# One-hot rows of later batches by eight narrow comparisons, tile one-hots one step later, and the first batch's masked gathers moved back

## The chip, the core and the metric

The kernel runs on one core of one Trainium2 chip. The metric is the device time of one execution in microseconds (us). Three runs of the kernel before gave a median of 1613.91 us (1612.84 to 1618.62). Of this kernel, half a per cent (about 8 us) is about what a measurement can tell from no change.

## The reference, cut to what matters

```python
# x: (16, 512, 1024), mask: (16, 1024) of 0 and 1, Wq and Wo: (512, 512)
xt = transpose(x, (0, 2, 1))                       # (B, T, D)
q = xt @ Wq.T
qh = q.reshape(B, T, 8, 64).transpose(0, 2, 1, 3)  # queries, keys and values are the same
scores = einsum('bhqd,bhkd->bhqk', qh, qh) / sqrt(64)
logits = (scores * cmask + (1 - cmask) * -1e30) * rmask
ctx = softmax(logits, axis=-1) @ qh
out = ctx.reshape(B, T, D) @ Wo.T
return x + transpose(out, (0, 2, 1))
```

A masked token is left out as a key. As a query, all its logits are zero, so its output is the mean of all tokens' values, one row for the whole batch.

## The kernel before, in words

**Tiles.** In each of the 16 batches the unmasked tokens are put first. They fit into 5 tiles of 108 rows (540 places, the form called "small"; the code also holds a form "middle" with 116 rows and a form "full", which these inputs don't use). The masked tokens follow in 5 tail tiles. Gathers by GpSimd's indirect DMA fetch the rows of x in this order (`small_xg` for the first five tiles, `small_xtail` for the tail), by the row numbers in `small_idx`; scatters write them back.

**Row numbers.** `idx` of a batch is a product on TensorE (`late_order`, line 1138): for each of 8 token groups (TT = 8) a one-hot matrix of the row within a tile (`late_hot_row`, 128 x 108, fp16) times a one-hot of the tile, weighted with the token's number (`late_hot_tile`). The tile one-hots of all batches are made once by two VectorE operations (`hot_tiles`, lines 901 and 904). The row one-hots are made for one batch at a time by `hot_row_of(b)` (line 933), with two buffers: one comparison of 864 elements a partition between `late_rowno` and `late_jl`, both broadcast. Batch 1's is made before the main loop, those of batches 2 to 15 in batch 0, at the steps in `HOT_ROW_AT`. VectorE then turns each product into `small_idx` (line 940).

**Main loop.** A batch is 8 heads of 5 steps, and (h, k) is step k of head h. In a step TensorE computes two half tiles of scores for the row maxima of the head after next (`max_scores`, line 1182; two PSUM banks, each given back by a VectorE reduction, line 962), two half tiles of scores of this head (lines 1198 and 1201), the products with the values one head later (line 1213), and pieces of other work on two PSUM banks called misc: projections of later pairs of heads (line 1248), transposes, the orders, and from the second batch on the previous batch's output. ScalarE takes the exponentials (line 812). GpSimd adds up the exponentials for the softmax's sums (`add_tile`, line 634: `small_Pacc`, 108 x 540), sums tokens (line 622), makes the low parts of Wo in batch 0 (`wo_low`, line 608) and issues the gathers and scatters (lines 568 and 580). Each float32 operand is a high part (rounded, `small_H`) and a low part (the rest, `small_L`), for which reason VectorE subtracts (line 977) behind ScalarE's copy (line 733).

**Order.** Each engine's order is written out by tables of steps: `WO_HIGH_AT` (ScalarE's high parts of Wo, line 685), `WO_LOW_AT` (GpSimd's low parts), `GATHER_TAIL_AT`, `SCATTER_AT`, `HOT_ROW_AT` and `ORDER_AT`. Engines wait for each other by semaphores only. SyncE's queue carries the copies of the high and low parts into the operand slots (`small_ops<-small_H` and `small_L`, 6 of 135 KB a head).

**Front.** Before batch 0 the list `front_jobs` is worked off: five transposes, the projections (0, 0) and (0, 1) of the first pair of heads, the two value transposes V, the projections (1, 0) and (1, 1), with the order of batch 1 between them, then (2, 0), and the row maxima of heads 0 and 1. `hot_tiles` stands behind the low part of (0, 0), `hot_row_of(1)` behind that of (0, 1). The batches' numbers for VectorE (`late_jl`, `late_rowno`, `late_boff`) are copied ahead of that (line 926). The projection (2, 0) writes the same buffer of `small_H` as pair 0, so ScalarE waits there until the copies of heads 0 and 1 have landed.

Of the kernel before, what the change touches and what calls it, by code (L numbers as in the profile page):

```python
# [19 lines left out]
P = 128  # L20
F32 = mybir.dt.float32
F32R = mybir.dt.float32r
BF16 = mybir.dt.bfloat16
F16 = mybir.dt.float16
I32 = mybir.dt.int32
ALU = mybir.AluOpType
# [26 lines left out]
SCALE_AT = [(3, 0), (3, 1)]  # L53
MASKED_AT = [(0, 0), (0, 1)]

WO_HIGH_AT = [(0, 3), (0, 4), (1, 0), (1, 1)]
WO_LOW_AT = [(1, 3), (1, 4), (2, 0), (2, 1)]

ADD_W_AT = [(0, 0), (0, 1), (0, 3), (0, 4), (1, 0)]
SCATTER_TAIL_AT = [(1, 1), (1, 3), (1, 4), (2, 0), (2, 1)]  # L60
GATHER_TAIL_AT = [(2, 3), (2, 4), (3, 0), (3, 1), (3, 3)]
SCATTER_AT = [(3, 4), (4, 0), (4, 1), (5, 0), (5, 1)]
# [102 lines left out]
def pool_jobs(form, has_prev, has_next, has_third):  # L165


    NT, NTAIL = form.NT, form.NTAIL
    table = {(h, k): [] for h in range(HEADS) for k in range(NT)}
    steps = list(table)  # L170
    if form.split:
        for i in range(NTAIL):
            if has_prev:
                table[ADD_W_AT[i]].append(("add_w", -1, i))
                table[SCATTER_TAIL_AT[i]].append(("scatter", -1, NT + i))
            table[GATHER_TAIL_AT[i]].append(("gather", 0, NT + i))
            table[TAIL_SUM_AT[i]].append(("sum_tokens", 0, NT + i))
        for i in range(NT):
            if has_prev:
                table[SCATTER_AT[i]].append(("scatter", -1, i))  # L180
            if has_third:
                table[GATHER_AT[i]].append(("gather", 2, i))
        for i in range(1, NT):
            if has_next:
                table[SUM_AT[i - 1]].append(("sum_tokens", 1, i))
            if not has_prev:
                table[FIRST_SUM_AT[i - 1]].append(("sum_tokens", 0, i))
        if not has_prev:
            for i, at in enumerate(WO_LOW_AT):
                table[at].append(("wo_low", 0, i))  # L190
        return table
    scatters = [steps[steps.index(at) + 2] for at in FULL_OUT_AT]
    gathers = [max(steps[steps.index(at) + 2], (1, 4)) for at in scatters]
    if has_prev:
        for i, at in enumerate(scatters):
            table[at].append(("scatter", -1, i))
    if has_next:
        for i in range(NT):
            table[gathers[i]].append(("gather", 1, i))
    for i in range(1, NT):  # L200
        table[4 + (i - 1) // 3, (i - 1) % 3].append(("sum_tokens", 0, i))
    return table
# [97 lines left out]
def attention_kernel(nc, x_rows, mask_t, wq, wqT, woT, out_rows, B, T, D):  # L300
    KD = D // P
    TT = T // P
# [4 lines left out]
    with ExitStack() as ctx:  # L307
# [6 lines left out]
        def sem(name):  # L314
# [24 lines left out]
            g_kept, place_step, onehots_made, perm_made, idx_made, jidx_made, ops_cleared = sems.values()  # L339
# [41 lines left out]
        for f, t in zip(forms, tensors):  # L381
# [17 lines left out]
            def place_tables(stage, t=t, f=f):  # L399

                batches = 1 if f.split else B
                tables = ExitStack()
                for where, name, shape, dt in (
                        ("early", "hot_tile_f", [P, TT, B, f.NTALL], F32), ("early", "jh", [P, TT, B], F32),
                        ("early", "jl", [P, TT, B], F32), ("early", "tileno", [P, f.NTALL], F32),
                        ("early", "tileno_i", [P, f.NTALL], I32), ("early", "rowno", [P, f.R], F32),
                        ("early", "rowno_i", [P, f.R], I32), ("early", "jidx_i", [P, f.NTALL], I32),
                        ("early", "boff_i", [P, B, f.NTALL], I32), ("early", "boff", [P, B, f.NTALL], F32),
                        ("early", "hot_tile", [P, TT, batches, f.NTALL], F16), ("early", "hot_row", [P, TT, batches, f.R], F16),
                        ("late", "late_jl", [P, TT, B], F32), ("late", "late_rowno", [P, f.R], F32),  # L410
                        ("late", "late_boff", [P, B, f.NTALL], F32), ("late", "late_hot_tile", [P, TT, B, f.NTALL], F16),
                        ("late", "late_hot_row", [P, 2, TT, f.R], F16)):
                    if where == stage:
                        t[name] = sb(f"{f.name}_{name}", shape, dt, tables)
                tables.close()
# [433 lines left out]
        def _(dve):  # L849
# [25 lines left out]
            def body(f, t, plan):  # L875
# [52 lines left out]
                def hot_row_of(b):  # L928

                    if b == 1:  # L930
                        dve.wait_ge(place_step, NTALL + 8)
                    at_least(dve, perm_made, b - 1)
                    nc.vector.tensor_tensor(t["late_hot_row"][:, b % 2], t["late_rowno"][:].unsqueeze(1).to_broadcast([P, TT, R]),
                                            t["late_jl"][:, :, b].unsqueeze(2).to_broadcast([P, TT, R]),
                                            ALU.is_equal).then_inc(onehots_made, 1)

                def idx_of(b, bank):

# [121 lines left out]
                for name, arg, bank, before in plan[0]:  # L1060
# [3 lines left out]
                    job(name, arg, bank, -1 if name == "xT" else 0, 1 if name == "xT" else 0, 0)  # L1064
                    if f.split and (name, arg) == ("xT", NT - 1):
                        move_tables()
                    if f.split and (name, arg) == ("proj", (0, 0)):
                        hot_tiles(t["late_hot_tile"])
                    if f.split and (name, arg) == ("proj", (0, 1)):
                        hot_row_of(1)  # L1070
                for m in range(2 * NT):
                    reduce_max(1, 1, m)
# [342 lines left out]
```

## Time and profile before

| | |
|---|---|
| median of three runs | 1613.91 us |
| the profiled execution's own time | 1613.59 us |
| its span, first to last instruction | 1611.8 us |
| TensorE matmuls busy | 1535.3 us (95%) |
| VectorE busy | 1190.2 us (74%) |
| ScalarE busy | 854.6 us (53%) |
| GpSimd busy | 1340.9 us (83%) |
| granted TensorE clock, mean | 0.977 of full |

Busy shares are means over the whole span. The first batch and the front are where they say least, so stretches are read one by one below. Idle time of an engine that nobody waits for costs nothing. In the rows PE is TensorE's matmuls, PEld its weight loads, DVE VectorE, ACT ScalarE, POOL GpSimd.

### The profile page before, as it was taken

The numbers are of one execution on the slowest core, as the hardware profiler recorded it, in microseconds if no ns is written. First come the engines' busy times: TensorE is split into PE (matmuls) and PEld (weight loads), VectorE is DVE, ScalarE is ACT, GpSimd is POOL, SyncE is SP. The second block draws the span as 40 slices with busy tenths as digits, with TensorE's granted clock in tenths as the row PEclk, the third lists the DMA queues.
The fourth block names the chain that finished last, engine by engine and source line by source line (L and its number), as shares of the span: only waits on it lengthen the run. The fifth ranks groups of instructions, "written<-read, shape, count | busy, mean of one in ns | idle before, by whom it ended". The sixth has DMA issues, their size and how long they took to land. (4 is left out here: it accounts for less than half of the span.)

```text
span 1611.8 us, 33099 instructions
## 1 busy us (share of the span) xinstructions
PE 1535.3 (95%) x10956; PEld 1218.7 (76%) x10956; DVE 1190.2 (74%) x2676; ACT 854.6 (53%) x2061; POOL 1340.9 (83%) x1078
## 2 busy tenths in 40 slices
PE   5989999999999999999999999999999999999984
PEld 4668787778777777777777777877777787778753
DVE  4587787878778787877878787777878777787743
ACT  4345555555555555555555555555555555655440
POOL 3467889898988989898898989889898988988864
PEclk9889999999999999999999999999999999999987
DMA  4433354454535445454544455454445444443501
GB/s 136 103 84 88 94 131 102 124 122 115 136 93 132 99 121 123 121 130 97 128 104 120 117 128 123 103 127 107 118 115 131 117 110 120 113 118 88 134 18 54
DMA packets 93810, 179.09 MB, mean 111 GB/s; under 512 B 24704, under 2 KB 24832, under 8 KB 93632
## 3 DMA queue, kind: packets, MB, share of 16 engines
q1 hardware_dynamic: 64448, 109.71, 29.4%
q0 software_dynamic: 29184, 67.17, 15.1%
q8 instruction: 92, 1.51, 0.4%
q14 instruction: 86, 0.70, 0.1%
HBM read 36.77 MB, written 33.55 MB: 44 GB/s over the span
## 5 line engine op out<-in xcount | busy, mean ns | idle before, releaser
L962 DVE TENSOR_REDUCE small_mxp<-max_scores 108x1 f32<-108x270 f32 x1280 | 547.9, 436 | 266.7 <-PE max_scores L1182 243.3
L812 ACT ACTIVATE small_Pt<-scores,small_kbias 108x270 f32<-108x270 f32 x1280 | 551.5, 483 | 363.3 <-PE scores L1201 357.9
L634 POOL TENSOR_TENSOR small_Pacc<-small_Pacc,small_Pt 108x540 f32<-108x540 f32 x384 | 520.7, 1356 | 124.0 <-ACT small_Pt L812 117.5
L1182 PE MATMUL max_scores<-small_ops 128*108 128x270 f32 x1280 | 417.9, 333 | 16.0 <-DVE small_mxp L962 14.2
L1213 PE MATMUL ctx_psum<-small_Pt,small_V 108*64 108x270 f32 x2560 | 317.6, 395 | 0.0
L994 DVE RECIPROCAL small_rsum<-small_rsum 128x67 f32<-128x67 f32 (+1 forms) x512 | 240.7, 532 | 78.7 <-ACT small_rsum L748 73.4
L1182 PEld LDWEIGHTS max_scores<-small_ops 128*108 128x108 f32 x1280 | 220.6, 175 | 86.5 <-issue 42.1
L1198 PE MATMUL scores<-small_ops 128*108 128x270 f32 x1280 | 271.3, 292 | 2.7 <-ACT small_Pt L812 2.7
L1213 PEld LDWEIGHTS ctx_psum<-small_Pt,small_V 108*64 108x64 f32 x2560 | 186.1, 139 | 111.1 <-issue 5.7
L1201 PE MATMUL scores<-small_ops 128*108 128x270 f32 x1280 | 265.7, 289 | 0.0
L1198 PEld LDWEIGHTS scores<-small_ops 128*108 128x108 f32 x1280 | 192.9, 174 | 21.8 <-issue 8.3
L634 POOL TENSOR_TENSOR small_Pacc<-small_Pt 108x540 f32<-108x540 f32 x128 | 171.8, 1342 | 31.5 <-ACT small_Pt L812 28.9
L1201 PEld LDWEIGHTS scores<-small_ops 128*108 128x108 f32 x1280 | 192.7, 174 | 0.0
L1248 PE MATMUL misc<-small_xcT,small_wqT_hi 128*128 128x270 f32 x512 | 151.8, 297 | 13.2 <-DVE small_xcT_lo L986 12.1
L1248 PE MATMUL misc<-small_xcT_lo,small_wqT_hi 128*128 128x270 f32 x512 | 148.6, 290 | 0.0
L1248 PE MATMUL misc<-small_xcT,small_wqT_lo 128*128 128x270 f32 x512 | 147.9, 289 | 0.0
L1248 PE MATMUL misc<-small_woT_hi,small_ctxT 128*108 128x512 f32 x320 | 127.0, 397 | 6.2 <-DVE small_ctxT_lo L999 6.2
L1248 PE MATMUL misc<-small_woT_lo,small_ctxT 128*108 128x512 f32 x320 | 127.5, 398 | 0.0
L1248 PE MATMUL misc<-small_woT_hi,small_ctxT_lo 128*108 128x512 f32 x320 | 126.7, 396 | 0.0
L1017 DVE TENSOR_TENSOR small_ctx<-small_rsum,ctx_psum 64x270 f32<-64x270 f32 x256 | 110.5, 432 | 9.1 <-issue 3.3
L568 POOL DMA_INDIRECT small_xg<-x_rows,small_idx x80 | 85.1, 1063 | 37.9 <-issue 15.3
L709 ACT CAST small_xcT<-misc 128x432 fp32r<-128x432 f32 x80 | 41.7, 521 | 134.8 <-PE misc L1260 134.8
(115 smaller groups left out, 2365.2 us busy)
## 6 DMA issues: line engine op xcount, KB each, us to landing
small_ops<-small_H SPq DMA_DIRECT2D x512, 135.0 KB
small_ops<-small_L SPq DMA_DIRECT2D x256, 135.0 KB
small_ops<-small_mrow SPq DMA_DIRECT2D x128, 2.1 KB
small_xg<-x_rows,small_idx POOLq DMA_INDIRECT x80, 4.0
small_xtail<-x_rows,small_idx POOLq DMA_INDIRECT x80, 4.6
out_rows<-small_xtail,small_idx POOLq DMA_INDIRECT x80, 3.7
out_rows<-small_xg,small_idx POOLq DMA_INDIRECT x80, 3.8
wqT_sb<-wqT SPq DMA_DIRECT2D x1, 1024.0 KB, 5.4
```

Of the source, the lines that this page charges most:

```text
L568: nc.gpsimd.indirect_dma_start(out=tokens(f, t, b, k), out_offset=None, in_=x_rows, in_offset=bass.IndirectOffsetOnAxis(ap=t["idx"][:r, b, ...
L634: nc.gpsimd.tensor_tensor(acc, other, t["Pt"][:R, p0], ALU.add).then_inc(pacc_step, 1)
L709: nc.scalar.copy(t["xcT"][:, :, R * arg:R * arg + R], MB[bank][:, 0:KD * R].rearrange("p (c r) -> p c r", c=KD)).then_inc(xT_kept, 1)
L812: nc.scalar.activation(t["Pt"][:R, (NT * s + k) % f.NP, half, :], ST[(2 * (NT * h + k) + half) % 3][:R, 0:H], ACT.Exp, bias=t["kbias"][:R, ...
L962: nc.vector.tensor_reduce(t["mxp"][:R, h % 2, m // 2, m % 2:m % 2 + 1], MX[m % 2][:R, 0:H], AX.X, ALU.max).then_inc(mx_red, 1)
L994: nc.vector.reciprocal(t["rsum"][:, cols], t["rsum"][:, cols]).then_inc(recip_step, 1)
L1017: last = nc.vector.tensor_tensor(t["ctx"][pr:pr + DK, h // 2 % 2, cols] if f.split else t["ctxT"][pr:pr + DK, h // 2, cols], t["rsum"][r0: ...
L1182: nc.tensor.matmul(MX[m % 2][:R, 0:H], ops[:, OPA, tile_cols(m // 2)], ops[:, OPB, half_cols(m % 2)], start=True, stop=True).then_inc(mx_r ...
L1198: nc.tensor.matmul(banks[half][:R, 0:H], ops[:, OPA, tile_cols(k)], ops[:, OPB, half_cols(half)], start=True, stop=False)
L1201: nc.tensor.matmul(banks[half][:R, 0:H], ops[:, OPY, tile_cols(k)], ops[:, OPX, half_cols(half)], start=False, stop=True).then_inc(s_ready, 1)
L1213: last = nc.tensor.matmul(CT[DK * half:DK * half + DK, 0:H], t["V"][:R, (h // 2) % 2, k, DK * (h % 2):DK * (h % 2) + DK], t["Pt"][:R, (NT ...
L1248: last = nc.tensor.matmul(out, lefts[a][left_at], rights[z][right_at], start=(c == 0 and i == 0), stop=(c == KD - 1 and i == 2))
```

## The change: what it does

Three edits. (1) `hot_row_of` compares a fp16 row of 108 numbers (`late_rowno` is now fp16) with a number per partition, eight times, once for each token group; the semaphore moves with the last. (2) In the front both `hot_tiles` and `hot_row_of(1)` now stand behind the low part of projection (0, 1). (3) Steps are moved: in batch 0 the five gathers of the masked tail are issued at the steps of `SCATTER_AT`, where there is no scatter yet, the high parts of Wo move on ScalarE, and the low parts on GpSimd. Later batches keep their steps.

```diff
-WO_HIGH_AT = [(0, 3), (0, 4), (1, 0), (1, 1)]
-WO_LOW_AT = [(1, 3), (1, 4), (2, 0), (2, 1)]
+WO_HIGH_AT = [(0, 2), (0, 4), (1, 1), (1, 3)]
+WO_LOW_AT = [(1, 0), (1, 3), (2, 0), (2, 3)]
...
-            table[GATHER_TAIL_AT[i]].append(("gather", 0, NT + i))
+            table[(GATHER_TAIL_AT if has_prev else SCATTER_AT)[i]].append(("gather", 0, NT + i))
...
-                        ("late", "late_jl", [P, TT, B], F32), ("late", "late_rowno", [P, f.R], F32),
+                        ("late", "late_jl", [P, TT, B], F32), ("late", "late_rowno", [P, f.R], F16),
...
-                    nc.vector.tensor_tensor(t["late_hot_row"][:, b % 2], t["late_rowno"][:].unsqueeze(1).to_broadcast([P, TT, R]),
-                                            t["late_jl"][:, :, b].unsqueeze(2).to_broadcast([P, TT, R]),
-                                            ALU.is_equal).then_inc(onehots_made, 1)
+                    for tt in range(TT):
+                        last = nc.vector.tensor_scalar(t["late_hot_row"][:, b % 2, tt], t["late_rowno"][:],
+                                                       t["late_jl"][:, tt, b:b + 1], None, ALU.is_equal)
+                    last.then_inc(onehots_made, 1)
...
-                    if f.split and (name, arg) == ("proj", (0, 0)):
+                    if f.split and (name, arg) == ("proj", (0, 1)):
                         hot_tiles(t["late_hot_tile"])
-                    if f.split and (name, arg) == ("proj", (0, 1)):
                         hot_row_of(1)
```

**VectorE, the front.** The rows from the copy of `late_boff` on, before. `small_L` is the low part of a projection: (0, 0), (0, 1), (1, 0), then (1, 1) and (2, 0).

```order
L926 COPY small_late_boff<-small_boff 128x160
L977 TENSOR_TENSOR small_L<-misc,small_H 128x270
L901 TENSOR_TENSOR small_hot_tile_f<-small_tileno,small_jh 128x1280
L904 TENSOR_TENSOR small_late_hot_tile<-small_hot_tile_f,tokid 128x1280
L977 TENSOR_TENSOR small_L<-misc,small_H 128x270
L933 TENSOR_TENSOR small_late_hot_row<-small_late_rowno,small_late_jl 128x864
L977 TENSOR_TENSOR small_L<-misc,small_H 128x270
L940 TENSOR_TENSOR small_idx<-misc,small_late_boff 108x10
```

The same place in the changed kernel.

```order
L926 COPY small_late_boff<-small_boff 128x160
L978 TENSOR_TENSOR small_L<-misc,small_H 128x270 x2
L901 TENSOR_TENSOR small_hot_tile_f<-small_tileno,small_jh 128x1280
L904 TENSOR_TENSOR small_late_hot_tile<-small_hot_tile_f,tokid 128x1280
L934 TENSOR_SCALAR small_late_hot_row<-small_late_rowno,small_late_jl 128x108 x8
L978 TENSOR_TENSOR small_L<-misc,small_H 128x270
L941 TENSOR_TENSOR small_idx<-misc,small_late_boff 108x10
```

The low part of (0, 1) stands ahead of the tile one-hots now; one operation of 864 elements has become eight of 108.

**GpSimd, heads 1 and 2 of batch 0.** Before, from the last token sum of head 1's beginning on. A head has four adds into `small_Pacc`, of which the first reads `small_Pt` alone.

```order
L622 TENSOR_TENSOR small_xsum<-small_xsum,small_xg 108x512
L634 TENSOR_TENSOR small_Pacc<-small_Pt 108x540
L634 TENSOR_TENSOR small_Pacc<-small_Pacc,small_Pt 108x540 x2
L608 TENSOR_TENSOR small_woT_lo<-woT_sb,small_woT_hi 128x512
L634 TENSOR_TENSOR small_Pacc<-small_Pacc,small_Pt 108x540
L608 TENSOR_TENSOR small_woT_lo<-woT_sb,small_woT_hi 128x512 x2
L634 TENSOR_TENSOR small_Pacc<-small_Pt 108x540
L608 TENSOR_TENSOR small_woT_lo<-woT_sb,small_woT_hi 128x512
L634 TENSOR_TENSOR small_Pacc<-small_Pacc,small_Pt 108x540 x2
L568 DMA small_xtail<-x_rows,small_idx 108x512
```

The same heads in the changed kernel.

```order
L622 TENSOR_TENSOR small_xsum<-small_xsum,small_xg 108x512
L608 TENSOR_TENSOR small_woT_lo<-woT_sb,small_woT_hi 128x512
L634 TENSOR_TENSOR small_Pacc<-small_Pt 108x540
L634 TENSOR_TENSOR small_Pacc<-small_Pacc,small_Pt 108x540 x2
L608 TENSOR_TENSOR small_woT_lo<-woT_sb,small_woT_hi 128x512
L634 TENSOR_TENSOR small_Pacc<-small_Pacc,small_Pt 108x540
L608 TENSOR_TENSOR small_woT_lo<-woT_sb,small_woT_hi 128x512
L634 TENSOR_TENSOR small_Pacc<-small_Pt 108x540
L634 TENSOR_TENSOR small_Pacc<-small_Pacc,small_Pt 108x540 x2
L608 TENSOR_TENSOR small_woT_lo<-woT_sb,small_woT_hi 128x512
L634 TENSOR_TENSOR small_Pacc<-small_Pacc,small_Pt 108x540
```

The first low part of Wo has moved ahead of head 1's adds and the last one behind head 2's third; the gather of the tail is no longer in head 2.

## Rows read from the trace of the kernel before

**Rows 1.** The page: busy time of the engines, and the granted clock in 40 slices.
```profile
PE 1535.3 (95%) x10956; PEld 1218.7 (76%) x10956; DVE 1190.2 (74%) x2676; ACT 854.6 (53%) x2061; POOL 1340.9 (83%) x1078
...
PEclk9889999999999999999999999999999999999987
```

**Rows 2.** Busy time by windows, heads 0 to 4 of batches 0 and 1 (columns in the first line).
```profile
core 0: us, PE busy (x) PEld busy (x) DVE busy (x) ACT busy (x) POOL busy (x), PEclk, DMA share, GB/s
64.30:134.90 70.60, 60.88 (x469) 50.05 (x467) 57.55 (x119) 35.85 (x84) 47.41 (x34) 0.85 0.26 63
...
167.50:228.60 61.10, 60.38 (x440) 49.02 (x439) 48.69 (x107) 34.13 (x82) 51.93 (x43) 1.00 0.44 109
```

**Rows 3.** The same view, narrower windows of the front and batch 0.
```profile
80.00:100.00 20.00, 15.14 (x123) 11.92 (x119) 18.28 (x34) 7.52 (x18) 12.96 (x9) 0.83 0.20 44
100.00:120.00 20.00, 16.87 (x121) 12.65 (x121) 17.35 (x37) 8.37 (x21) 15.00 (x11) 0.80 0.45 114
120.00:140.00 20.00, 19.21 (x139) 15.90 (x140) 13.28 (x32) 11.34 (x28) 10.60 (x9) 0.86 0.25 60
88.00:90.00 2.00, 0.00 (x0) 0.00 (x0) 2.00 (x1) 0.00 (x0) 2.00 (x2) 0.51 0.55 122
42.00:44.00 2.00, 2.00 (x12) 2.00 (x12) 0.44 (x1) 0.38 (x1) 1.40 (x2) 0.59 0.91 226
```

**Rows 4.** The row one-hots, 0 to 150 us: busy us, mean ns; then min/median/max ns.
```profile
L933 DVE TENSOR_TENSOR small_late_hot_row<-small_late_rowno,small_late_jl 128x864 f16<-128x864 f32 x15 | 22.2, 1479 | 0.1
...
L933 DVE TENSOR_TENSOR small_late_hot_row<-small_late_rowno,small_late_jl x15: 1043/1068/4446, 33.2 to 117.7; 128x864 f16<-128x864 f32 x15
```

**Rows 5.** Timeline at 84 to 92 us: start us, duration us, engine, line; idle before in brackets.
```profile
85.41 1.27 POOL L608 TENSOR_TENSOR small_woT_lo<-woT_sb,small_woT_hi 128x512 fp32r<-128x512 f32 x1
85.65 4.45 DVE L933 TENSOR_TENSOR small_late_hot_row<-small_late_rowno,small_late_jl 128x864 f16<-128x864 f32 x1
...
86.65 1.32 POOL L634 TENSOR_TENSOR small_Pacc<-small_Pacc,small_Pt 108x540 f32<-108x540 f32 x1
...
87.93 3.30 POOL L608 TENSOR_TENSOR small_woT_lo<-woT_sb,small_woT_hi 128x512 fp32r<-128x512 f32 x2
...
90.24 0.88 PE L1138 MATMUL misc<-small_late_hot_tile,small_late_hot_row 128*108 128x10 f16 x8 [3.63 <-DVE small_late_hot_row L933]
```

**Rows 6.** Timeline, two other meetings of GpSimd's operations and the row one-hots.
```profile
73.94 2.31 POOL L634 TENSOR_TENSOR small_Pacc<-small_Pacc,small_Pt 108x540 f32<-108x540 f32 x1
73.98 1.05 DVE L933 TENSOR_TENSOR small_late_hot_row<-small_late_rowno,small_late_jl 128x864 f16<-128x864 f32 x1
...
107.11 1.00 POOL L568 DMA_INDIRECT small_xtail<-x_rows,small_idx  x1 [0.30 <-issue]
108.14 1.34 POOL L634 TENSOR_TENSOR small_Pacc<-small_Pt 108x540 f32<-108x540 f32 x1
108.16 2.24 DVE L933 TENSOR_TENSOR small_late_hot_row<-small_late_rowno,small_late_jl 128x864 f16<-128x864 f32 x1
```

**Rows 7.** Timeline of the front, 30 to 46 us, by engine.
```profile
30.62 0.38 ACT L733 CAST small_H<-misc 128x270 fp32r<-128x270 f32 x1 [1.11 <-PE misc L1248]
...
31.41 1.49 DVE L904 TENSOR_TENSOR small_late_hot_tile<-small_hot_tile_f,tokid 128x1280 f16<-128x1280 f32 x1
32.83 0.43 DVE L977 TENSOR_TENSOR small_L<-misc,small_H 128x270 fp32r<-128x270 f32 x1
...
33.40 0.41 PE L1296 MATMUL misc<-identR,small_H 128*108 128x128 f32 x1 [2.82 <-DVE small_L L977]
...
40.08 1.01 POOL L568 DMA_INDIRECT small_xg<-x_rows,small_idx  x1 [14.22 <-DVE small_idx L940]
...
45.47 0.39 ACT L733 CAST small_H<-misc 128x270 fp32r<-128x270 f32 x1 [2.22 <-DMA small_ops<-small_L]
```

**Rows 8.** Timeline of VectorE: short operations that follow each other without a wait.
```profile
27.25 0.21 DVE L926 COPY small_late_rowno<-small_rowno 128x108 f32<-128x108 f32 x1
...
27.38 0.24 DVE L926 COPY small_late_boff<-small_boff 128x160 f32<-128x160 f32 x1
...
90.56 0.16 DVE L940 TENSOR_TENSOR small_idx<-misc,small_late_boff 108x10 int32<-108x10 f32 x1
90.64 0.43 DVE L962 TENSOR_REDUCE small_mxp<-max_scores 108x1 f32<-108x270 f32 x1
```

## The prediction

> **What bounds the kernel now.** I read the page first. TensorE's matmuls are busy for 95% of the span, VectorE's work for 74%, and the granted clock is at its full level (2.4 GHz) in all slices but the first three and the last [rows 1]. So the long middle belongs to TensorE, and nothing in the change touches batches 1 to 15. What can move is the front and batch 0. Next I set heads 0 to 4 of batch 0 beside those of batch 1, by windows [rows 2]. Batch 0 takes 70.6 us for them, batch 1 61.1 us, though only batch 1 has the output product of the batch before in these heads. TensorE shows 60.9 us busy at a mean clock of 0.85 in batch 0, against 60.4 us at full clock: it idles 9.7 us and runs the rest partly at half clock. VectorE is at 57.6 of 70.6 us, and at 18.3 and 17.4 of 20 us between 80 and 120 us [rows 3]. This is the one stretch of the kernel where VectorE sets the pace.
>
> From the three 20 us windows the time at half clock (1.2 GHz) follows: 2 x (0.17 + 0.20 + 0.14) x 20 = 20.4 us [rows 3], three spells of some 6.8 us. Each costs the work that TensorE would have done in half of it, 3.4 us, 10.2 us in all. What stood before the first spell is plain: TensorE did nothing from 88 to 90 us, and its clock fell there [rows 3].
>
> Then I looked for who kept TensorE waiting. The 15 row one-hots take 22.2 us, 1.48 us in the mean, but 1.04 us at the least and 4.45 us at the most [rows 4]. 15 x 1.05 is 15.8 us, so 6.4 us of it is not work. The timeline shows what it is. The comparison that starts at 85.65 us meets GpSimd's operations at 85.41, 86.65 and 87.93 us, and ends when the third of these (the first of the two low parts of Wo) is over plus its own 0.95 us; the order on TensorE waits 3.63 us for it [rows 5]. At 108.16 us one waits 1.2 us behind an add into Pacc. At 73.94 us it is the other way round: the comparison takes its 1.05 us and the add 2.31 in place of 1.34 us [rows 6]. So this comparison and a GpSimd operation don't run at the same time, and whichever has begun is finished first.
>
> **The front.** The low part of projection (0, 1) starts at 32.83 us, behind the tile one-hots, though its high part is done at 30.62 + 0.38 = 31.00 us [rows 7]. It can start 1.83 us sooner, and with it V on TensorE and the first copies on SyncE's queue. Behind it VectorE has 2.9 us of tile one-hots and the first row one-hot, to about 35.1 us by my count from these rows, so order, index and batch 1's gathers start near 36 instead of 40.08 us. What ends last in the front is not VectorE: ScalarE's high part of (2, 0) at 45.47 us waits 2.22 us for the copies of heads 0 and 1 to land [rows 7], 12 x 135 KB = 1.66 MB, 7.3 us at the 226 GB/s of the fastest row here [rows 3]. These start 1.83 us sooner, but the five gathers (5 x 108 rows of 2 KB, 1.1 MB, 4.9 us at that rate) now start 4 us sooner and take a share of the DMA engines while the copies still run. Bounds: 0 where the gathers eat all of it, 3.0 us where the projections also stay at full clock because TensorE's gap of 2.82 us closes. I take 1.7 us, near the shift itself.
>
> **The eight comparisons.** No row shows this operation. From rows of short operations: an index (10 elements) is followed by the next start after 0.08 us, a float32 copy of 108 elements after 0.13 us [rows 8]. So 0.07 us is fixed and 0.06 us goes with 108 float32 elements. Bounds of eight: 8 x 0.075 = 0.60 us and 8 x 0.13 = 1.04 us, against 0.96 us for the one operation (1.04 us, less the 0.08 us by which the copy overlaps with the next). I take half the copy's slope for half the bytes, 0.10 us each, 0.80 us a group: 0.16 us saved, in 14 groups 2.2 us (bounds: 1.1 us lost, 5.0 us gained). Ten of the groups stand in the stretch where VectorE is short, so I put 1.6 us on the path. The Trainium skill (page "VectorE: DVE Perf Modes", section "The TRN2 errata") gives 58 cycles plus a quarter of the elements at 0.96 GHz for fp16 in SBUF with one tensor input, which would be 0.09 us each; by it the sum would gain another 0.9 us. No row here shows such an operation.
>
> **The meetings with GpSimd.** Of the 6.4 us, 3.4 us belong to one meeting, at 85.65 us. In the order of the changed kernel the same three GpSimd operations still stand behind each other at that step (low part of Wo, add, low part of Wo); only the fourth is gone. I therefore leave most of it in. The 1.2 us at 108.16 us go: that add was held until 108.14 us by the gather at 107.11 us, which is moved away. Of the rest I take half off. That makes 3.2 us less. Against it stands that a group is now eight operations with seven gaps. Where a GpSimd add becomes ready inside a group (as at 73.94 us), it can enter at a gap, and VectorE waits 1.34 us where before GpSimd waited. I expect two of these, 2.7 us. Net: 0.5 us gained.
>
> **The moved steps.** The tail gathers stand where later batches issue scatters, with sums 3 or 4 steps later, and batch 1 runs with full clock on the same density [rows 2], so I cost them at nothing; cover for them is GpSimd's idle time in heads 3 to 5 (10.6 of 20 us busy from 120 to 140 us [rows 3]). If a sum came too early for its gather, GpSimd would wait, and behind it only adds, which ScalarE needs eight tiles later. The casts on ScalarE are the same four; it is 7.5 of 20 us busy.
>
> **The clock.** With some 2 us less waiting in heads 1 to 3, I expect one of the three spells not to come, 3.4 us.
>
> **Sum.** 1.7 + 1.6 + 0.5 + 3.4 = 7.2 us. From the profiled execution, 1613.6 us (span 1611.8 and 1.8 around it, 0.3 below the median of the runs), this gives 1606.4; set against the median it is 1606.7. I say 1607.
>
> **Rivals.**
> Freed stretch: the meetings all but vanish, because a short operation slips in between GpSimd's and GpSimd's pile is thinner. Then 1.7 + 2.2 + 4.0 of the 6.4 us and two spells (6.8 us) go: 14.7 us, 1599. For it: TensorE has 60.9 us busy in 70.6 at a clock of 0.85, so some 19 us are there to win at most (half of the 20.4 us and the 9.7 us idle). Against it: the three operations still stand in a row at the worst place.
>
> GpSimd enters every group (the slower side): each of the 14 groups is cut once by an add of 1.34 us, 18.8 us, in place of the 6.4 us; with 1.7 and 2.2 us gained that is 1613.6 + 18.8 - 6.4 - 3.9 = 1622. It breaks even at 7.7 entries. For it: GpSimd is busy 13 to 15 of 20 us there [rows 3], and holds the comparison off for three operations in a row at 85.65 us [rows 5]. Against it: only four or five adds of before became ready inside a comparison, and the group is shorter. The Trainium skill speaks for this rival: page "SBUF — State Buffer", section "Who interferes with whom", says that a VectorE operation with two SBUF inputs collides with a GpSimd operation that reads SBUF, and that a one-input operation in a two-port mode (`tensor_scalar` on fp16 can enter it) collides with any GpSimd operation, descriptor writing included, each held for a whole instruction. The trace agrees on the first half (2.31 for 1.34 us [rows 6]); on the second it has nothing.
>
> Nothing much: the comparison is at its upper bound (1.04 us) and the gathers eat the front's gain. Only the meeting at 108.16 us and small change remain: about 1612.
>
> **Chances.** The forecast's case 0.45 (its own range 1602 to 1611); freed stretch 0.27; GpSimd enters more than eight groups 0.13; nothing much 0.15. Faster by over 0.5% (below 1605.8; half a per cent is about what a measurement tells from no change): nearly all of the freed case and a quarter of the first, 0.38. Slower by over 0.5% (above 1622.0): the far end of the third, 0.05. Within: 0.57. The range leaves out the lower third of the freed case and the upper half of the third rival: 1598 to 1616.
>
> **What would show it.** Low part of (0, 1) at about 31.0 us, first gather of batch 1 near 36 us, high part of (2, 0) near 43.8 us. Eight comparisons in about 0.80 us; 0.96 us or more would sink the second term. Whether a comparison in a group lasts over 1 us, and which GpSimd operation it meets; at the step of the old 85.65 us I expect a wait again. Time at half clock in heads 0 to 4 of 13 to 14 us instead of 20.4. Heads 5 to 7 and all later batches must be as long as before; if they change, or the tail sums wait for gathers, the prediction is wrong in a part that I cost at nothing.

## The result and the profile after

The changed kernel is slower: 1625.8 us median of six runs (1623.63 to 1630.03) against 1615.3 us of the kernel before, also of six runs on the same chip. The ratio is 1.0064, with a 95% interval of 1.0048 to 1.008. The forecast was 1607 us, and the range ended at 1616. The profiled execution has a span of 1624.9 us, 13.1 us more than before.

The first view is busy time by windows again: heads 0 to 4 of batch 0, the same heads of batch 1, the three 20 us windows, and two of 2 us (columns as in [rows 2]).

```profile
64.50:148.50 84.00, 66.21 (x469) 54.10 (x468) 70.32 (x216) 35.76 (x84) 40.04 (x32) 0.80 0.21 49
181.00:242.10 61.10, 60.38 (x441) 49.03 (x439) 48.52 (x107) 34.15 (x83) 51.92 (x43) 1.00 0.44 109
...
80.00:100.00 20.00, 13.71 (x98) 11.00 (x97) 19.11 (x59) 7.40 (x18) 8.26 (x7) 0.78 0.19 43
100.00:120.00 20.00, 15.55 (x94) 11.43 (x92) 16.48 (x57) 6.22 (x15) 6.61 (x6) 0.67 0.18 43
120.00:140.00 20.00, 16.80 (x110) 13.48 (x111) 14.39 (x46) 9.08 (x21) 8.82 (x8) 0.70 0.28 65
...
88.00:90.00 2.00, 0.00 (x0) 0.00 (x0) 2.00 (x2) 0.00 (x0) 2.00 (x3) 1.00 0.88 196
90.00:92.00 2.00, 0.00 (x0) 0.00 (x0) 2.00 (x3) 0.00 (x0) 1.89 (x2) 0.75 0.94 211
```

Heads 0 to 4 of batch 0 went from 70.6 us [rows 2] to 84.0 us. That is 13.4 us, the whole of the difference between the spans; batch 1's took 61.1 us before and after, heads 5 to 7 of batch 0 take 32.5 us (32.6 before) and all behind batch 1's head 4 1382.8 us (1383.2). VectorE is busy 70.3 us there, 12.8 us more than before. TensorE has the same 469 matmuls in it, busy 66.2 us against 60.9, and stands idle 17.8 us against 9.7: 5.3 us of the loss are matmuls at the lower clock, 8.1 us are waiting. The clock: the three windows give 2 x (0.22 + 0.33 + 0.30) x 20 = 34 us at half clock (1.2 GHz), against 20.4 us [rows 3]. TensorE does nothing from 88 to 92 us, and within that time its clock falls: 1.00 in the first two us, 0.75 in the mean of the next two.

The second view is the timeline of VectorE, the row one-hots alone (start us, duration us). One row is a group of eight comparisons. The 14 groups of batch 0:

```profile
64.41 1.35 DVE L934 TENSOR_SCALAR small_late_hot_row<-small_late_rowno,small_late_jl 128x108 f16<-128x108 f16 x8
69.98 4.13 DVE L934 TENSOR_SCALAR small_late_hot_row<-small_late_rowno,small_late_jl 128x108 f16<-128x108 f16 x8
76.36 2.49 DVE L934 TENSOR_SCALAR small_late_hot_row<-small_late_rowno,small_late_jl 128x108 f16<-128x108 f16 x8
81.07 2.48 DVE L934 TENSOR_SCALAR small_late_hot_row<-small_late_rowno,small_late_jl 128x108 f16<-128x108 f16 x8
86.75 5.81 DVE L934 TENSOR_SCALAR small_late_hot_row<-small_late_rowno,small_late_jl 128x108 f16<-128x108 f16 x8
93.96 1.36 DVE L934 TENSOR_SCALAR small_late_hot_row<-small_late_rowno,small_late_jl 128x108 f16<-128x108 f16 x8
96.19 1.35 DVE L934 TENSOR_SCALAR small_late_hot_row<-small_late_rowno,small_late_jl 128x108 f16<-128x108 f16 x8
99.78 1.47 DVE L934 TENSOR_SCALAR small_late_hot_row<-small_late_rowno,small_late_jl 128x108 f16<-128x108 f16 x8
107.64 4.61 DVE L934 TENSOR_SCALAR small_late_hot_row<-small_late_rowno,small_late_jl 128x108 f16<-128x108 f16 x8
113.64 1.36 DVE L934 TENSOR_SCALAR small_late_hot_row<-small_late_rowno,small_late_jl 128x108 f16<-128x108 f16 x8
115.88 1.35 DVE L934 TENSOR_SCALAR small_late_hot_row<-small_late_rowno,small_late_jl 128x108 f16<-128x108 f16 x8
119.47 1.46 DVE L934 TENSOR_SCALAR small_late_hot_row<-small_late_rowno,small_late_jl 128x108 f16<-128x108 f16 x8
125.82 3.58 DVE L934 TENSOR_SCALAR small_late_hot_row<-small_late_rowno,small_late_jl 128x108 f16<-128x108 f16 x8
130.79 1.40 DVE L934 TENSOR_SCALAR small_late_hot_row<-small_late_rowno,small_late_jl 128x108 f16<-128x108 f16 x8
```

Two things stand in these rows. A group that nothing disturbs takes 1.35 us, longer than the 1.05 us that the operation it replaces takes undisturbed (1.04 at the least [rows 4]). And six groups take much more. The 14 sum to 34.2 us; 14 x 1.35 is 18.9, so 15.3 us are waits, against 6.4 us before. TensorE feels it in its orders (groups by line, 0 to 150 us, before, then changed; the last figures are TensorE's idle time ahead of them and what ended it):

```profile
L1138 PE MATMUL misc<-small_late_hot_tile,small_late_hot_row 128*108 128x10 f16 x120 | 9.6, 204 | 5.5 <-DVE small_late_hot_row L933 5.5
```

```profile
L1138 PE MATMUL misc<-small_late_hot_tile,small_late_hot_row 128*108 128x10 f16 x120 | 10.9, 215 | 15.3 <-DVE small_late_hot_row L934 15.3
```

Third, what the longest group meets (timeline, 86 to 93 us, VectorE, GpSimd and the order on TensorE):

```profile
86.75 1.42 POOL L634 TENSOR_TENSOR small_Pacc<-small_Pacc,small_Pt 108x540 f32<-108x540 f32 x1 [3.25 <-ACT small_Pt L812]
86.75 5.81 DVE L934 TENSOR_SCALAR small_late_hot_row<-small_late_rowno,small_late_jl 128x108 f16<-128x108 f16 x8
88.14 1.26 POOL L608 TENSOR_TENSOR small_woT_lo<-woT_sb,small_woT_hi 128x512 fp32r<-128x512 f32 x1
89.36 1.32 POOL L634 TENSOR_TENSOR small_Pacc<-small_Pacc,small_Pt 108x540 f32<-108x540 f32 x1
90.64 1.26 POOL L608 TENSOR_TENSOR small_woT_lo<-woT_sb,small_woT_hi 128x512 fp32r<-128x512 f32 x1
...
92.71 0.50 PE L1138 MATMUL misc<-small_late_hot_tile,small_late_hot_row 128*108 128x10 f16 x4 [5.81 <-DVE small_late_hot_row L934]
```

Four GpSimd operations, two adds and two low parts of Wo, run inside one group, and TensorE's order waits 5.81 us. The group stands at step (1, 3). Before, the comparison of that step had already begun when the add became ready, and it was the add that was held (timeline of the kernel before, 80 to 86 us):

```profile
83.21 1.04 DVE L933 TENSOR_TENSOR small_late_hot_row<-small_late_rowno,small_late_jl 128x864 f16<-128x864 f32 x1
83.83 1.61 POOL L634 TENSOR_TENSOR small_Pacc<-small_Pacc,small_Pt 108x540 f32<-108x540 f32 x1 [2.94 <-ACT small_Pt L812]
```

Now the add goes in at the gap behind the first of the eight. Then the engines take turns: of the next three comparisons one waits for one operation, one for two, one for one again, and the last low part is over as VectorE goes on to the fifth. Step (1, 4), where the pile of [rows 5] stood, has the undisturbed group at 93.96 us.

Last, the front (timeline: VectorE's second low part, GpSimd's first gather of batch 1, ScalarE's high part of (2, 0)):

```profile
30.89 0.44 DVE L978 TENSOR_TENSOR small_L<-misc,small_H 128x270 fp32r<-128x270 f32 x1 [1.06 <-ACT small_H L733]
...
37.44 1.01 POOL L568 DMA_INDIRECT small_xg<-x_rows,small_idx  x1 [11.44 <-DVE small_idx L941]
...
46.19 0.39 ACT L733 CAST small_H<-misc 128x270 fp32r<-128x270 f32 x1 [6.86 <-DMA small_ops<-small_L]
```

The second low part is 1.94 us sooner than in [rows 7], the gather 2.64 us sooner, and the high part that the front ends on 0.72 us later. ScalarE now waits 6.86 us for the copies. These are times of one execution; in this one the DMA engines were also busy to only 0.36 from 34 to 36 us, while one copy's issue on SyncE took 2.00 us (32.66 to 34.66 us) in place of 0.6. Why it did is not known.

### The profile page after: what moved, and what is told of

It is laid out like the page before. It is cut to its first block and busy times, and to the rows that moved or that the text cites. A ratio compares the mean times of both kernels' runs of the same rounds, so it can differ in the third digit from the quotient of the medians.

```text
span 1624.9 us, 33204 instructions
## 1 busy us (share of the span) xinstructions
PE 1536.4 (95%) x10956; PEld 1219.8 (75%) x10956; DVE 1202.2 (74%) x2781; ACT 854.3 (53%) x2061; POOL 1335.8 (82%) x1078
## 5 line engine op out<-in xcount | busy, mean ns | idle before, releaser
L1248 PE MATMUL misc<-small_xcT,small_wqT_hi 128*128 128x270 f32 x512 | 150.9, 295 | 13.5 <-DVE small_xcT_lo L987 12.1
```

Of the source, the lines that this page charges most:

```text
L1248: last = nc.tensor.matmul(out, lefts[a][left_at], rights[z][right_at], start=(c == 0 and i == 0), stop=(c == KD - 1 and i == 2))
```

## The experiments

Ratios are to the kernel before, of runs on the same chip, with a 95% interval. Where a short diff is shown, it is against the changed kernel, and shortened. Waits of VectorE are told as before: what the 14 groups of batch 0 took, less 14 undisturbed ones.

### Each part by itself

**One comparison, all else changed.** The single float32 operation, with its float32 row, is put back into the changed kernel.

```diff
-for tt in range(TT):
-    last = nc.vector.tensor_scalar(t["late_hot_row"][:, b % 2, tt], t["late_rowno"][:], t["late_jl"][:, tt, b:b + 1], None, ALU.is_equal)
+nc.vector.tensor_tensor(t["late_hot_row"][:, b % 2], rowno broadcast, jl broadcast, ALU.is_equal).then_inc(onehots_made, 1)
```

> The changed kernel with the single comparison of 864 elements (float32 row) put back; tile one-hots behind the second low part and all moved steps kept. Theory 'comparisons' (eight narrow ones are slower, 1.27 us a group against 0.96, and GpSimd's operations enter between them): the whole loss of 10 to 13 us goes, ratio to before 0.998 to 1.001, row one-hots back to about 1.0 us with one or two meetings. Theory 'moved steps' (the low parts of Wo or the gathers at their new steps cost it): the loss stays, ratio 1.005 to 1.008.

Ratio 0.9993 (0.9977 to 1.0009). The whole loss is gone. The row one-hots (groups by line, 0 to 150 us):

```profile
L933 DVE TENSOR_TENSOR small_late_hot_row<-small_late_rowno,small_late_jl 128x864 f16<-128x864 f32 x15 | 21.7, 1448 | 0.1
```

That is 0.5 us less than before [rows 4]: the moved steps took hardly any of the old waits away (6.0 us in place of 6.4). The wait at 108.16 us is gone, others have come: five groups wait over 0.4 us, where one or two were expected.

**Eight comparisons alone.** Against the kernel before, only `hot_row_of` and the fp16 row.

> The kernel before with the eight comparisons (fp16 row) alone; front and steps as before. 'Comparisons': slower by 8 to 16 us, ratio 1.005 to 1.010, groups of 1.27 us when alone and 1.1 to 1.3 us more for each GpSimd operation met. 'Moved steps': within 3 us of before, ratio 0.998 to 1.002.

Ratio 1.0107 (1.0086 to 1.0128), slower by some 17 us: more than the whole change, and a little more than either theory expected. So the comparisons are the cause, and in their company the other edits help: without them it is 7 us worse. Its trace has 19.0 us of waits against 15.3 us, with a group of 7.03 us at step (1, 3), where a third low part of Wo stands in the pile.

**Front alone.** Against the kernel before, only `hot_tiles` behind (0, 1).

> The kernel before with the tile one-hots behind the second low part alone. Theory 'landing' (the copies of heads 0 and 1 share the DMA engines with batch 1's gathers, which start sooner): the second low part starts 2 us sooner, the high part of (2, 0) not sooner than 45.5 us, time within 1 us of before. Theory 'front gains': high part of (2, 0) near 43.8 us and 1.5 to 2 us gained over the kernel.

Ratio 0.9999 (0.9988 to 1.0011). The second low part starts at 30.67 us, 2.2 us sooner, and ScalarE's high part of (2, 0) hardly sooner:

```profile
45.12 0.39 ACT L733 CAST small_H<-misc 128x270 fp32r<-128x270 f32 x1 [7.31 <-DMA small_ops<-small_L]
```

It waits 7.31 us for the copies. They are what the front ends on, and they start 2.2 us sooner and are waited for until 0.35 us sooner. 'Front gains' (43.8 us) is out and 'landing' fits, though 45.12 us is a little below its bound of 45.5. That it is the earlier gathers that hold the copies up is argued: the DMA engines are busy to 0.94 and more from 34 us on, but no run left the gathers late.

**Moves alone.** Against the kernel before, only the three edits of step tables.

> The kernel before with the moved steps alone (high and low parts of Wo, gathers of the masked tail). 'Comparisons': between 4 us faster and 1 us slower, since one GpSimd operation less stands behind the worst meeting; ratio 0.997 to 1.001. 'Moved steps': slower by 6 us or more, ratio over 1.004.

Ratio 0.9989 (0.9973 to 1.0005). If anything a gain; the interval includes no change.

### Pace and meetings

**Short GpSimd work, eight comparisons.** In heads 0 to 3 of batch 0 the adds are cut to 4 of 270 columns a half and the low parts to 8 of 512; the rest of these sums is left out.

```diff
-nc.gpsimd.tensor_tensor(acc, other, t["Pt"][:R, p0], ALU.add).then_inc(pacc_step, 1)
+nc.gpsimd.tensor_tensor(acc[:, :, 0:4], other[:, :, 0:4], t["Pt"][:R, p0, :, 0:4], ALU.add).then_inc(pacc_step, 1)   # heads 0 to 3 of batch 0
```

> The changed kernel with GpSimd's work made short where the comparisons are: in heads 0 to 3 of batch 0 the adds into Pacc take 4 of 270 columns a half, and the low parts of Wo 8 of 512 columns (the rest of the sums and low parts is left out). Theory 'meetings and pace' (GpSimd's long operations between the eight comparisons, and 0.16 us a comparison): every group near 1.27 us, and the time falls below before's by 3 to 10 us, ratio 0.994 to 0.998. Theory 'the comparisons themselves' (something else in them slows the stretch): groups short, but the time stays 6 us or more above before.

**The same with the single comparison.**

> The same short GpSimd work (same parts left out) with the single comparison of 864 elements. 'Meetings and pace': 4 to 6 us below the run with eight comparisons and short GpSimd work (14 x 0.30 us of pace and a little clock), ratio to before 0.990 to 0.995; this also says what the meetings cost the kernel before, 6 to 12 us. If the two short-GpSimd runs differ by 10 us or more, meetings are not what the change lost by.

Ratios 0.9998 (0.9981 to 1.0016) and 0.9972 (0.9951 to 0.9994). Groups by line, 0 to 150 us (busy us, mean ns of one), first with eight, then with one comparison:

```profile
L940 DVE TENSOR_SCALAR small_late_hot_row<-small_late_rowno,small_late_jl 128x108 f16<-128x108 f16 x120 | 20.3, 246 | 0.1
```

```profile
L939 DVE TENSOR_TENSOR small_late_hot_row<-small_late_rowno,small_late_jl 128x864 f16<-128x864 f32 x15 | 15.8, 1053 | 0.1
```

No waits are left in either (246 ns each against 370 ns in the changed kernel). The two differ by 0.0026, 4.2 us, which is what 14 groups of 0.30 us more would be. That is pace. 'Meetings and pace' had the groups and the difference of the two runs (4 to 6 us) right, but expected both kernels faster than they are: 0.994 to 0.998 for the eight, 0.990 to 0.995 for the one. 'The comparisons themselves' (6 us above before) is out. With full GpSimd work the two differ by 1.0064 - 0.9993 = 0.0071, 11.5 us. The rest, 7.3 us, is meetings: they cost the single comparison 0.9993 - 0.9972 = 0.0021 (3.4 us) and the eight 0.0066 (10.7 us). The shortened work takes part of GpSimd's own time away in both, so these are differences of the two, not costs of the meetings alone. The sizes are rough: by the intervals of the ratios the 4.2 us have some 4 us either way, the 7.3 us some 6.

**A float32 row.** Only the type of `late_rowno` differs.

> The changed kernel with the row of 108 numbers in float32 in place of fp16. If the element count and type set the pace of a comparison (0.158 us), it rises to 0.18 to 0.19 us and the time by 2 to 4 us over the changed kernel. If a fixed cost sets it, pace and time stay within 0.005 us and 2 us; ratio to before 1.005 to 1.010 in both.

Ratio 1.0129 (1.0105 to 1.0153). The undisturbed group in the front:

```profile
34.08 1.57 DVE L934 TENSOR_SCALAR small_late_hot_row<-small_late_rowno,small_late_jl 128x108 f16<-128x108 f32 x8
```

Eight take 1.57 us in place of 1.35, so one follows the other after 0.185 us instead of 0.158 us (from the start times of the rows). The type does count, 0.027 us for 108 elements. In 120 comparisons that is 3.2 us, but the time rose by 0.0065, 10.5 us, over the changed kernel, where 2 to 4 us were expected. The trace doesn't hold the reason: four of the five runs took 1633 to 1635 us at a mean granted clock of 0.968 to 0.971, the profiled one 1622.6 us at 0.980. This stays open.

**Eight comparisons with two inputs.** The number per partition is a broadcast second tensor, and the row is float32.

```diff
-("late", "late_rowno", [P, f.R], F16)
+("late", "late_rowno", [P, f.R], F32)
...
-nc.vector.tensor_scalar(t["late_hot_row"][:, b % 2, tt], t["late_rowno"][:], t["late_jl"][:, tt, b:b + 1], None, ALU.is_equal)
+nc.vector.tensor_tensor(t["late_hot_row"][:, b % 2, tt], t["late_rowno"][:], t["late_jl"][:, tt, b:b + 1].to_broadcast([P, R]), ALU.is_equal)
```

> The changed kernel with eight comparisons of 108 elements that have two tensor inputs (the number per partition broadcast along the row, float32 row). 'Seven gaps' (GpSimd enters because there are eight operations): as many meetings as in the changed kernel, 11 to 15, ratio 1.005 to 1.010. 'The kind of operation' (only the one-input form lets GpSimd in, or collides with more of GpSimd's operations): meetings as with the single comparison, 5 to 7, ratio 0.999 to 1.003. Pace near 0.17 us each by either.

Ratio 1.0072 (1.0043 to 1.0101), as slow as the changed kernel. Three of its groups, the first undisturbed:

```profile
65.96 1.53 DVE L934 TENSOR_TENSOR small_late_hot_row<-small_late_rowno,small_late_jl 128x108 f16<-128x108 f32 x8
71.51 6.78 DVE L934 TENSOR_TENSOR small_late_hot_row<-small_late_rowno,small_late_jl 128x108 f16<-128x108 f32 x8
...
110.51 4.85 DVE L934 TENSOR_TENSOR small_late_hot_row<-small_late_rowno,small_late_jl 128x108 f16<-128x108 f32 x8
```

The 14 sum to 34.2 us, of which 12.8 are waits; nine comparisons waited over 1 us each, near the 11 to 15 of 'seven gaps'. So GpSimd gets in without the one-input form: it is enough that there are eight with gaps between them. Whether the one-input form costs something on top is open. The run that differs from this one in nothing else is the float32 row: 1.0129 against 1.0072, at nearly the same pace (1.57 and 1.53 us), with 14.8 us of waits in its trace. The run times of either spread over 12 us with the clock, and their difference is not clear of that.

**Against a constant.** Eight more comparisons in the front, with the constant 5.0 as scalar.

> The changed kernel with eight more comparisons in the front, after the low part of (1, 1), where VectorE waits: the same fp16 row against a constant in place of the number per partition. If reading the number per partition is the dear part of the 0.130 us that the comparison costs beside its elements, these follow each other after 0.09 to 0.10 us; if the kind of operation is, after 0.158 us like the others. No effect on the time is expected by either.

Run once, for the pace alone (timeline of VectorE in the front, first with the number per partition, then with the constant):

```profile
34.04 1.35 DVE L936 TENSOR_SCALAR small_late_hot_row<-small_late_rowno,small_late_jl 128x108 f16<-128x108 f16 x8
...
38.48 0.94 DVE L1070 TENSOR_SCALAR small_late_hot_row<-small_late_rowno 128x108 f16<-128x108 f16 x8
```

1.35 us against 0.94 us, and one of the constant's seven steps was held by a gather's issue (0.184 us). The other six are 0.096 us in the mean, from start to start, against 0.158 us: about 0.06 us of each comparison is the number per partition. With a constant the pace is near 0.10 us, the price that I had put in.

### Other ways to make the rows

**Packed fp16.** One operation of 864 elements, rows by token groups, all fp16 with innermost step 1.

```diff
+nc.vector.tensor_tensor(t["late_hot_row"][:, b % 2] as [P, R, 4, 2], rowno pair broadcast over 4, late_jl[:, b] as [4, 2] broadcast over R, ALU.is_equal)
-nc.tensor.matmul(bank, t["late_hot_row"][:, b % 2, tt, :], ...)
+nc.tensor.matmul(bank, t["late_hot_row"][:, b % 2, :, tt], ...)
```

> The changed kernel with one comparison of 864 elements, all operands fp16 and laid out so that the innermost step is 1 everywhere (rows by token groups; TensorE reads the one-hots with a step of 8). 'Pace and meetings': if two-byte operands halve the slope, a group takes about 0.5 us with two inputs in one operation, has 3 to 6 meetings, and the time is 4 to 8 us below the single float32 comparison with the same steps, ratio 0.995 to 0.998. If the slope stays 1.04 ns an element: 0.97 us, ratio 0.998 to 1.001. If strided weights cost TensorE, its order products take over 0.2 us each.

Ratio 1.0006 (0.9997 to 1.0016). VectorE's part came as hoped, 594 ns at the least, but TensorE's weight loads of the orders did not (groups by line, 0 to 150 us, this kernel, then the kernel with the single float32 comparison):

```profile
L1141 PEld LDWEIGHTS misc<-small_late_hot_tile,small_late_hot_row 128*108 128x108 f16 x120 | 25.0, 292 | 1.5 <-issue 1.5
```

```profile
L1137 PEld LDWEIGHTS misc<-small_late_hot_tile,small_late_hot_row 128*108 128x108 f16 x120 | 9.5, 156 | 8.0 <-issue 6.7 <-DVE small_idx L940 1.2
```

Read with a step of 8, a load takes 292 ns in place of 156: 15.5 us more of weight loads, which ate the gain. The runs by pairs below, with a step of 2, bear this out.

**Low parts of Wo apart**, single float32 comparison.

```diff
-WO_LOW_AT = [(1, 0), (1, 3), (2, 0), (2, 3)]
+WO_LOW_AT = [(1, 1), (2, 1), (3, 1), (4, 0)]
```

> The single float32 comparison with the changed kernel's front and gathers, and GpSimd's low parts of Wo at steps (1,1), (2,1), (3,1), (4,0), where no row one-hot is made. 'Meetings': the pile at head 1's last step goes (3.16 us to 1.0 to 2.3 us), 2 to 5 us gained over the same kernel with the changed steps, ratio 0.996 to 0.999. 'Meetings don't matter': ratio 0.999 to 1.001.

Ratio 0.9999 (0.9987 to 1.0011). The pile shrank (3.23 us to 2.13 us at that group), without effect on the time; 'meetings' expected 2 to 5 us. **Packed and apart** together:

> The packed fp16 comparison and the low parts of Wo at the steps without a one-hot, together. 'Pace and meetings': the fastest of all, 6 to 12 us below before, ratio 0.992 to 0.997. 'Meetings don't matter' and a slope of 1.04 ns: ratio 0.999 to 1.001.

Ratio 1.0012 (0.9999 to 1.0026), where 0.992 to 0.997 was expected: a miss as well. It has fewer waits than any other kernel with GpSimd's whole work, 2.1 us, and the same weight loads of 292 ns.

**By pairs of token groups.** One fp16 operation again, laid out [4, R, 2]: TensorE reads with a step of 2.

> The changed kernel with one fp16 comparison of 864 elements laid out by pairs of token groups, so that TensorE reads the one-hots with a step of 2 instead of 8. 'Pace and meetings': VectorE's groups as in the packed version (0.52 us when alone), TensorE's weight loads of the orders near 0.16 us again, time 2 to 6 us below the single float32 comparison with the same steps, ratio 0.995 to 0.998. 'VectorE's time for the one-hots is covered below about 1 us a group': ratio 0.998 to 1.001, and the loss of the change comes only from what goes beyond.

Ratio 0.9966 (0.9948 to 0.9984). **Pairs, low parts apart:**

> The same with GpSimd's low parts of Wo at the steps without a row one-hot. 'Pace and meetings': 5 to 10 us below before, ratio 0.993 to 0.997, at most two meetings over 0.5 us. 'Covered below about 1 us': ratio 0.998 to 1.001.

Ratio 0.9944 (0.9922 to 0.9966): 1605.19 us median, about 9 us less than before. The time is as 'pace and meetings' expected, though four groups wait over 0.5 us and not two. This one beats both kernels. Its rows (groups by line, 0 to 150 us):

```profile
L936 DVE TENSOR_TENSOR small_late_hot_row<-small_late_rowno,small_late_jl 128x864 f16<-128x864 f16 x15 | 13.5, 899 | 0.1
L1141 PEld LDWEIGHTS misc<-small_late_hot_tile,small_late_hot_row 128*108 128x108 f16 x120 | 9.5, 151 | 2.1 <-issue 2.0
```

13.5 us for 15 groups against 22.2 us [rows 4], and weight loads at 151 ns. The run to set beside it has the same steps and the single float32 comparison, 0.9999. So VectorE's time is paid in both directions here; that it is covered below 1 us is out.

## Why the prediction was wrong

**What bounds.** Right: only heads 0 to 4 of batch 0 moved, VectorE sets the pace there, and half clock comes on top. (The granted clock is below 0.9 in the last two slices of [rows 1], not in the last alone, and the first slice is not below it. Nothing hangs on that.)

**The eight comparisons** (1.6 us gained) is the first step that failed. I priced the operation at 0.10 us, between 0.075 and 0.13 us, from a copy and from an index operation. Neither reads a number per partition. It measured 0.158 us, beyond my upper bound: 0.096 us with a constant, as priced, and 0.06 us for that number. A group undisturbed takes 0.30 us more than the one operation, not 0.16 less: 4.2 us of loss in 14 groups, and as much by the two runs with short GpSimd work. The page "VectorE: DVE Perf Modes" of the Trainium skill, section "The TRN2 errata", gave 0.09 us; that is near what the constant measured, and the number per partition is not in it, so the measurement decides. The same page of the Trainium skill has one-input operations move four 16-bit elements a cycle and two float32 ones (section "The perf-mode tier table"). The 0.027 us by which the two row types differ agree with that: 27 cycles at its 0.96 GHz are 0.028 us.

**The meetings** (0.5 us gained) is the second, and the larger. I expected two entries of GpSimd for 2.7 us and 3.2 us less of the old waits. From the start times of the 112 comparisons in batch 0, twelve waited over 1 us each, one of them for two GpSimd operations; waits rose from 6.4 to 15.3 us. The old waits did not shrink either: with the single comparison and the same moved steps they are 6.0 us. I had the mechanism, an entry at a gap, but counted only adds that had become ready inside a comparison before. What I missed is that VectorE and GpSimd can take turns: once GpSimd has entered, its next operation is ready too, so each may cost one more wait, as the four in the 5.81 us group. I also did not ask who had paid until then. GpSimd's 20 adds and four low parts in these heads took 36.5 us before and take 32.2 us now, where they would take 31.8 us unheld (1.34 and 1.26 us each). So GpSimd, for which other engines waited 0.7 us in these heads before, has lost its waits, and VectorE, which sets the pace, has got them.
The rival "GpSimd enters every group" had this sign, and its break-even of 7.7 entries was passed; its 1622 us was nearest to the result. It too was wrong in shape: 6 of 14 groups were held for over 1 us, some by several operations, and I gave it the least chance of all.
The page "SBUF — State Buffer" of the Trainium skill (section "Who interferes with whom") names the one-input two-port form as one that collides with any GpSimd operation. This case doesn't need it: with two inputs, eight narrow operations lost as much (1.0072). Nor does the trace show a whole-instruction hold where GpSimd writes descriptors: a gather's issue of 1.00 us lies inside the group at 130.79 us, and the group took 1.40 us, 0.05 more than undisturbed.

```profile
130.86 1.00 POOL L568 DMA_INDIRECT small_xtail<-x_rows,small_idx  x1 [0.30 <-issue]
```

**The front** (1.7 us gained): its lower bound, 0, was right and my value wrong. The shift came (30.89 us), the landing did not (46.19 us; alone 45.12 us, ratio 0.9999). The front's length also differs by more than I forecast from one execution to the next: the first row one-hot of batch 0 starts at 64.24 us before, at 64.41 us in the changed kernel, and at 63.46 and 65.96 us in two others with the same front (one comparison; two inputs).

**The clock** (3.4 us gained): the half-clock time of heads 0 to 4 grew from 21.2 us (2 x 0.15 x 70.6) to 33.6 us (2 x 0.20 x 84.0) in place of shrinking, which cost 5.3 us of TensorE's time. This followed from the waits above: within the 5.81 us wait the clock fell.

**The moved steps** at nothing: right within what can be told (0.9989 alone), and with the front 7 us to the good beside eight comparisons. **The pile** stayed, as forecast, but a step earlier than I said: it holds the group of (1, 3) for 5.81 us, and that of (1, 4), the old 85.65 us, not at all. Heads 5 to 7 and later batches did not change.

In sum, 7.2 us were to be gained, and the span grew by 13.1 us. On VectorE the two terms that failed make it up: 4.2 us of pace and 8.9 us of waits. On TensorE the same stretch reads as 8.1 us of idle time and 5.3 us of lower clock; these are two views of one loss and are not to be added.

## What to carry to other kernels

Before one operation is cut into several narrow ones on an engine that shares something with another engine, price the gaps: each gap is a place where the other may go first, for its whole operation. Ask which of the two held the other until now: waits that cost nothing on one engine can cost their full length on the other. Take the price of an operation only from rows that have its operands; a scalar read per partition (0.06 us) was dearer here than what fp16 elements save against float32 ones (0.027 us for 108). And where VectorE sets the pace, shorten it by packing types within one operation, then look at what its layout does to the reader.

## What the runs showed of the hardware that was not expected

- A comparison with a number per partition costs 0.06 us more than with a constant (0.158 us against 0.096 us from start to start).
- Of two engines that hold each other off, neither is sure to go next when an operation ends: in the 5.81 us group comparisons waited for one, two and one GpSimd operations, and before, one comparison waited for three in a row [rows 5].
- A TensorE weight load of 128 x 108 fp16 took 156 ns with step 1, 151 ns with step 2 (4 bytes) and 292 ns with step 8 (16 bytes).
- One 864-element comparison took 1.04 us with float32 inputs and 0.59 us with fp16 ones at step 1, two inputs in both.
